# Half of a routing chain moved into the first attention stage of a two-batch decoder block on one Trainium2 core

## The reference, cut to what matters

```
x = x + L0_attn(layernorm(x))            # causal attention, 16 heads in 4 groups
x = x + L0_xattn(ctx, layernorm(x))      # each token attends to a window of 4 context rows
x = x + L0_ffn(layernorm(x))             # 8 experts, top 2, with a capacity, FFN width 896
x = x + L1_attn(layernorm(x))            # attention with relative positions
x = x + L1_xattn(layernorm(x), ctx)
x = x + L1_ffn(layernorm(x))
```

## Time and profile before

| | |
|---|---|
| three runs | 1757.22, 1758.69, 1758.92 us; median 1758.69 |
| the profiled execution | 1761.55 us, of which the span of the trace is 1759.8 us |
| `attention0` with its opening | 0 to 361 us |
| `experts`: lead, batch 0's chain | 362 to 428 us |
| `experts`: batch 1's chain up to the first item | 428 to 463 us |
| `experts`: items 0 and 1 with the rest of that chain | 463 to 552 us |
| `experts`: the other items, then the join | 552 to 870 us, 870 to 953 us |
| `attention1`, `tail` | 953 to 1590 us, 1590 to 1760 us |

### The profile page before, as it was taken

How to read it: one execution, slowest core, us unless ns; L and a number is a source line. 1 busy time by engine, 2 the same in 40 slices (tenths; PEclk the granted TensorE clock), 3 DMA queues, 4 the chain that set the end, 5 groups by cost and what they waited for, 6 DMA issues and landing times. The chain is left out here.

```text
span 1759.8 us, 34234 instructions
## 1 busy us (share of the span) xinstructions
PE 1564.3 (89%) x12792; PEld 1071.0 (61%) x12792; DVE 1014.5 (58%) x2073; ACT 887.0 (50%) x1480; POOL 563.5 (32%) x817
## 2 busy tenths in 40 slices
PE   7689989878479999999975899999999999997988
PEld 3333333256368766776753577777777777775544
DVE  6577777335332111111166888888788888873566
ACT  5256656732331111111134788888788888873321
POOL 4311111122313000000253355555555565542111
PEclk9799999987779999999997899999999999998899
DMA  5811111030123133221237797886868778544101
GB/s 161 235 25 24 24 27 21 1 132 19 42 75 132 63 120 128 87 87 60 61 96 187 214 224 203 199 212 195 208 191 201 201 201 210 172 133 172 49 12 36
DMA packets 209796, 213.06 MB, mean 121 GB/s; under 512 B 19651, under 2 KB 187217, under 8 KB 209505
## 3 DMA queue, kind: packets, MB, share of 16 engines
q1 hardware_dynamic: 199969, 192.52, 40.3%
q0 software_dynamic: 4864, 13.64, 2.3%
q10 hardware_dynamic: 4800, 4.72, 0.8%
HBM read 128.82 MB, written 81.81 MB: 120 GB/s over the span
## 5 line engine op out<-in xcount | busy, mean ns | idle before, releaser
L1353 DVE CUSTOM_DVE_ANT_0 prob<-ps,dev 128x1024 f32<-128x1024 f32 x256 | 311.6, 1218 | 3.0 <-DMA skew_p<-prob 2.9
L1246 ACT ACTIVATE prob<-prob,nmax 128x1024 f32<-128x1024 f32 x256 | 293.2, 1146 | 7.5 <-DVE nmax L1353 7.3
L1162 PE MATMUL ps<-cst,prob 128*128 128x128 f32 x2048 | 278.8, 277 | 0.1
L2048 PE MATMUL ps<-xeT,w 128*128 128x384 f32 (+2 forms) x896 | 256.3, 448 | 5.1 <-DVE hT L2252 4.4
L1162 PEld LDWEIGHTS ps<-cst,prob 128*128 128x128 f32 x2048 | 227.7, 141 | 42.3 <-issue 21.0
L1381 DVE COPY probT<-ps 128x512 f32<-128x512 f32 x256 | 176.4, 689 | 101.5 <-PE ps L1162 101.5
L868 ACT ACTIVATE pT<-ps 128x512 f32<-128x512 f32 (+3 forms) x384 | 166.1, 495 | 118.3 <-PE ps L824 115.9
L906 DVE TENSOR_REDUCE nmax<-ps 128x1 f32<-128x128 f32 (+7 forms) x256 | 184.0, 753 | 70.7 <-PE ps L803 69.5
L2048 PEld LDWEIGHTS ps<-xeT,w 128*128 128x128 f32 x896 | 177.0, 198 | 77.8 <-DVE hT L2252 4.8
L2112 ACT ACTIVATE xT_c<-ps 128x256 f32<-128x256 f32 (+2 forms) x98 | 46.6, 476 | 326.3 <-PE ps L2048 326.2
L1255 ACT ACTIVATE probT<-ps 128x512 f32<-128x512 f32 x256 | 151.3, 591 | 101.2 <-PE ps L1162 101.0
(11 more groups left out here) (322 smaller groups left out, 2284.5 us busy)
## 6 DMA issues: line engine op xcount, KB each, us to landing
dev<-skew_u SPq DMA_DIRECT2D x128, 256.0 KB, 3.5
skew_p<-prob SPq DMA_DIRECT2D x128, 256.0 KB, 3.4
w<-in_L_ffn_w SPq DMA_DIRECT2D x20, 896.0 KB, 6.3
skew_u<-cst SPq DMA_DIRECT2D x64, 256.0 KB, 4.0
pre<-skew_p SPq DMA_DIRECT2D x128, 128.0 KB, 2.9
qs<-qd SPq DMA_DIRECT2D x72, 128.0 KB, 3.8
vz<-in_L_ffn_w SPq DMA_DIRECT2D x10, 896.0 KB, 5.6
ks1firsta<-kd SPq DMA_DIRECT2D x24, 256.0 KB, 5.7
```

What stands on the lines that cost most here:

```text
L1162: last = nc.tensor.transpose(ps[:, ring_bank(job), kb * P:(kb + 1) * P], prob_tile(t, (4 * h + kb) * P, (4 * h + kb + 1) * P), k.c("ident"))
L1246: nc.scalar.activation(prob_tile(t, 0, S), prob_tile(t, 0, S), ACT.Exp, bias=nmax[:, t % 4:t % 4 + 1], scale=-1.0).then_inc(s_exp, 1)
L1353: nc.vector.tensor_tensor_reduce(out=prob_tile(t, 0, S), in0=scores, in1=dev_tile(t), scale=-1.0, scalar=3.0e38, op0=ALU.add, op1=ALU.min, ...
L2048: last = nc.tensor.matmul(ps[:, a + z * wide + h, 0:cols], w[:, j, c, f * P:(f + 1) * P], xeT[:, c, h * cols:(h + 1) * cols], start=(c == ...
```

## The change

Five things are done.

1. `with_chain` inserts batch 0's chain (46 steps, and its 16 scatters) into `attention0`'s list, behind ("heads", 3, 0): the 62 entries are spread evenly over the keys from there to the sixth from the end. Its order is `early_order`, which puts the steps of both token halves behind one another. The rows and the chain's PE steps share the two slots of PSUM banks 0 to 3 (`tenants`, `claim_slot`). `wo` and the gate weights are loaded in `attention0`.
2. `experts` therefore begins with batch 1's chain, up to ("shift", 2). Then comes ("rows", 0), and the rest of the chain is dealt among items 0 and 1, one and two PE steps behind an `ffn` in turn, two behind a `y`. The 72 `warm` matmuls are gone. `AHEAD` is 5, which makes 15 items of 14 and 11 sets of weights of 10.
3. The last wait on `proj.stored` leaves `experts`: SP waits for it in `attention1`, before the loads of its second group, and DVE before a memset of the padding of `prob`, which moves behind the projection.
4. At the join, the last five `low` units move from DVE to POOL, behind the last gather; the first loads of q parts are issued after six units, not eight; on ACT `middles(KB - 1)` stands before `normed(3)`.
5. In `attention1`'s projection ACT does `middle` of the unit before, then `high`, then the store of the unit before (it was high, middle, and the store of two units before), and DVE does `low` before `residue`.

```diff
+def with_chain(steps, chain, after, upto):
+    extra = list(chain.order) + [("scatter", t, c) for t in range(KB) for c in range(2)]
+    at = steps.index(after) + 1
+    keys = [i for i, s in enumerate(steps) if s[0] == "key" and i >= at][:-upto]
+    out, given = list(steps[:at]), 0
+    for i in range(at, len(steps)):
+        out.append(steps[i])
+        if i in keys:
+            while given * len(keys) < len(extra) * (keys.index(i) + 1):
+                out.append(("chain", extra[given]))
+                given += 1
...
+            steps = with_chain(attention_steps(cells, G, 8), chain, ("heads", KVH - 1, 0), 6)
...
+            tenants = [s for s in steps if s[0] == "row" or s[0] == "chain" and s[1][0] in RowChain.SINGLE]
+            slot = {s: 2 * (x % 3 if x < M else x % 2) for x, s in enumerate(tenants)}
...
+                        if step[0] == "chain" and step[1][0] in RowChain.SINGLE:
+                            if step[1] == ("turn", 0, 0):
+                                pe.wait_ge(s_out, 2 * KVH)
+                            chain.inputs_ready(pe, step[1])
+                            claim_slot(step)
+                            chain.tensor(pe, step[1], ps[:, slot[step], :])
...
+def early_order(b):
...
+    return ([("turn", g, 0), ("turn", g, 1), ("prep", b), ("out", g, 0), ("out", g, 1), ("turn", h, 0), ("turn", h, 1), ("out", h, 0),
+             ("out", h, 1)] + both("stat") + both("shift") + four("norm") + both("hid") + both("pos") + both("mask") + both("score") +
+            both("sum") + both("flip") + four("value") + both("stat", 4) + both("shift", 4) + four("norm", 4) + both("logit") +
+            [("best", b), ("cum", b), ("slot", b)])
...
-    begun = chain.index(("hid", 3)) + 1
+    begun = chain.index(("shift", 2))
     under = list(chain[begun:])
-    order = list(lead) + list(chain[:begun]) + [("rows", 0)]
+    order = list(chain[:begun]) + [("rows", 0)]
...
             order.append(("ffn", n, f))
-            deal()
+            deal(1 + f % 2)
...
-    AHEAD = 4
+    AHEAD = 5
...
-                    if i == 8:
+                    if i == 6:
...
-                proj.stored(sp)
...
+                for n in range(5, KB):
+                    for i in proj.of(n):
+                        proj.low(pool, i)
```

More of the change, by code:

```diff
@@ L946, in attention1 @@
+            k.end_stage()
+        experts(k, out, chain)
+        k.sems += spanning
 def attention1(k):
@@ L1802, in warmed, with experts_order, deal @@
     return [s for step in steps for s in ([("warm", where[step], step)] if step in where else []) + [step]]
-def experts_order(items, lead, chain, ahead):
-    begun = chain.index(("hid", 3)) + 1
+def experts_order(items, chain):
+    begun = chain.index(("shift", 2))
     under = list(chain[begun:])
-    order = list(lead) + list(chain[:begun]) + [("rows", 0)]
-    def deal():
+    order = list(chain[:begun]) + [("rows", 0)]
+    def deal(few):
         singles = 0
-        while under and singles < 2:
+        while under and singles < few:
             order.append(under.pop(0))
@@ L1824, in experts_order, with experts @@
         order.append(("y", n))
-        deal()
+        deal(2)
     assert not under
     return order
-def experts(k, heads):
+def experts(k, heads, early):
     nc, ps, x = k.nc, k.ps, k.x
-    AHEAD = 4
+    AHEAD = 5
     EVEN = CAP // P * P
@@ L2164, in _ @@
                 rooted(3)
+                middles(KB - 1)
                 normed(3)
-                middles(KB - 1)
                 turned(3)
```

612 lines of the change are left out of this document (319 added, 293 removed).

## The result

Over six runs the changed kernel took 1749.05 us in the median (1741.52 to 1754.82), the kernel before, run beside it, 1758.81. The ratio is 0.9941 with a 95% interval of 0.9926 to 0.9956: faster by 0.6%, some 10 us. The forecast had the sign and its range holds the time, but it said 38 us.

A forecast was written before the change was run, and what follows sets the result against it. PE bounds attention and later experts' items; latency bounds the hole between, 362 to 552 us. Attention +50, experts -82, join -7, item boundary +1: -38 us, from the median 1758.69 to 1721 us; range 1692 to 1752.

The forecast's parts named there:

- Part 2: Experts, up to ("ffn", 2, 0): 108 us against 190, so 82 us saved; range 65 to 96 saved.
- Part 1: First attention, taking batch 0's chain: 50 us longer; floor 24, upper end 74.
- the prediction's own sign of being wrong: Attention growing by over 74 us or under 24, or the experts' first stretch taking over 125 us.
- the term of PE: First attention: of 34 us of chain work at full clock, 10 fit PE's idle time, 24 can't be hidden.
- the three other terms: First attention: 11 us for DVE, 5 for ACT's table loads, 10 for dependences between steps.
- The loads' 5 us: First attention: eight ACT table loads, 10.3 us in four blocks, stop PE for about 5 us; ends 0 and 10.3.
- DVE's 11: First attention: of 35 us of DVE chain work 11 don't fit and add to PE's share; ends 0 and 35.
- The scatters: First attention, group 7: 20 us on POOL cost nothing, as a mask waits at most one scatter; 10 without cover.
- The join: Experts to `attention1`: 7 us saved, about 5.5 from the store wait, 2 in `attention1`'s front, less 0.5 for the memset.
- The items: Experts: one more item boundary costs 1 us; its rows and `y` are otherwise the same work.
- The drain that the Trainium skill puts behind each table load: Rival, first attention: each of eight switches holds ACT and PE another 1.28 us; part 1 60, 1731 us; chance 0.05.
- The rival in which the chain stops the attention at every step: First attention: 46 steps each stop PE 0.6 us, nothing hides; 102 us, total 1773, deciding from 88; chance 0.13.

The follow-up runs named there:

- the run at a clock of 0.97: Changed kernel plus 236 identity transposes in the first attention, wherever PE stood idle or ran narrow matmuls: 1749.72 us, ratio 0.9949.
- the one in which PE's busy time rose by 16 us more and the stretch by 14: Changed kernel with 236 identity transposes, plus two more behind each value step of groups 4 to 7: 1762.88 us, ratio 1.0018.
- the run that was 17 us slower: Changed kernel with two scatters to an entry, so 54 entries over the same keys: 1766.53 us, ratio 1.0039.
- the repeat: The changed kernel run once more with no edit: 1748.81 us, ratio 0.9941.

## Why the prediction was right and wrong

**Part 2, the experts, was right, and nearly to the microsecond:** 82.8 us saved where 82 were forecast; the new stretch took 107.4 us, and 106 to 108 in four other executions of the same code, where 108 were forecast. Two of its terms can be read: PE stood 5.26 us for the first `rows` (4 forecast), and the granted clock of the stretch was 0.82. The other terms were not measured one by one, so luck may have part in the sum. No chain step of `experts` waits for a scatter any more.

**Part 1 was wrong, and it is nearly the whole error.** The stretch grew by 77 us in the profiled execution, and by 75 in two others, where 50 were forecast and 74 was the upper end; that was the prediction's own sign of being wrong. The step that failed is the term of PE: "Of 34 us, 24 can't be hidden." It failed in both of its halves.

- The 34 took the clock at the 1.00 of the earlier trace rows and kept it there. The work was about that, as the run at a clock of 0.97 shows (35.5). But in this trace the clock fell behind stops of several microseconds and in or just behind the logit steps that the chain brought, and PE's new busy time was 51 to 54 us. That makes 17 to 20 of the missing 25 to 27 us.
- The 10 us of idle time that this work was to fill were hardly filled: idle time grew by 23 to 24 us, where the three other terms, 26 us, less those 10 made 16. That makes the other 7 to 8.

Busy and idle time are measured. That the clock's 17 to 20 us lie on the path rests on several runs together: the one that put 28 us of transposes in at no cost, the one in which PE's busy time rose by 16 us more and the stretch by 14, the one in which 6 to 9 us of PE's work less were worth 9, and the 14 us at 0.50 without a pause. No run has the clock without the transposes, so this price is worked out, not measured by itself, and slack at the chain's steps remains as a rival.

The other terms held in the main. The loads' 5 us were about 5. DVE's 11 were of the right kind: PE's waits for the row maxima grew by 10 us, and ten instructions of the masks alone gave 7. The scatters, put at nothing, were not nothing: the waits for POOL's masks grew by 3.4 us. "A mask waits at most one scatter of 1.27 us" left out that the first scatter itself waits on POOL for the slot step, with a mask behind it.

**The small terms.** The join gave 4.4 us where 5 were forecast, but not for the reason given: the wait on the stores is worth 0.5 us, not 5.5, and the earlier trace rows could not tell that wait from the barrier's own time. The waits of the earlier trace rows are gone; what that gave in the front of `attention1`, where 2 were forecast, can't be read from one execution, since all behind the barrier took 802 to 806 us in executions of the same code. The items cost 3.6 us, not 1: ("ffn", 2, 0) now starts at a low clock (15.1 us to its next part, as in the row above; the items behind it take 12.3), and there is one item more.

**The rivals.** The drain that the Trainium skill puts behind each table load ("ScalarE: Activation LUTs", section "What ACT_TABLE_LOAD costs") is refuted here by the rows of ACT, in this order of exponentials and roots too, and by the price of 5 us for all eight. The rival in which the chain stops the attention at every step went the way the kernel went, though not to its 88 us: in sum nothing of the chain was hidden, since 75 to 77 us is what the chain took alone, 69, and four more table loads, 5. That the sums agree does not show why: 17 to 20 us of it are the clock's. My argument against it, that an engine with two independent streams usually has one ready, did not hold here: each queue has one written order, and PE stood 5.4 us behind the second mask with attention work left.

## What to carry to other kernels

Here work put beside a stage whose fullest engine is at 90% cost that engine's time in full; cost it at the clock it will get and not at the clock of the stage before the change, and look in the trace for stops and for steps in which the clock fell. Before trusting "it fits into the idle time", compare with the time the moved chain takes alone: in this one case, with one written order for each queue, that was the better forecast. And look where each moved step lands in every queue: in the run that was 17 us slower, steps of an engine that is busy for a third of the time had come to stand ahead of masks that PE waits for.

## What the runs showed of the hardware

In the changed kernel the clock fell from 2.4 to 1.2 GHz behind idle time, and at 382 us also with PE at work (1.92 of the 2 us before): 16 matmuls of eight columns then took 3.55 us instead of 1.90. In the repeat the same sixteen took 1.92 us and the clock fell behind them, at 386 us, so the place is not fixed. Transposes of the identity took 0.12 us each (28.3 us for 236), and with them the clock stood at 1.00 from 231 to 396 us; two at a time behind a value step, 92 were busy for 21.3 us, 0.23 us each. A table load of ACT took 1.28 us with the next instruction 0.01 to 0.02 us behind it, among exponentials as well as at the earlier trace rows. While a scatter waited 9.96 us for its indices, the mask behind it in POOL's queue did not start: PE stood 2.85 us for it.
